# VectorE's order in a graph convolution, mixing weights without their zero columns

## The chip, the cores and the metric

The kernel runs on one core of a Trainium2 chip. The metric is the device time of one execution in microseconds (us); three runs of the kernel before took 1550.62, 1556.21 and 1556.63, median 1556.21. A profile was taken of another execution.

## The reference, cut to what matters

The model has two layers. Each is a convolution on a graph of 512 nodes, with three low-rank attentions, followed by a feed-forward part (experts in layer 0, ternary weights in layer 1). For each of 16 batch items, with x of 512 nodes, 16 channels and 12 times:

```python
x_res = _conv2d(jnp.swapaxes(x, 1, 2), res_w, res_b, STRIDE, 0)
xc = ...
xt = ...
s = _attention(xt, W1_s, W2_s, False)
h = jnp.einsum('bnm,bmct->bnct', s * A[None], xt)
g = jnp.einsum('bnct,cf->bnft', h, W_gcn)
y = _conv2d(jnp.swapaxes(g, 1, 2), tcn_w, tcn_b, STRIDE, 1) + x_res
y = jax.nn.relu(y)
z = jnp.transpose(y, (0, 3, 2, 1))
mu = z.mean(-1, keepdims=True)
var = ((z - mu) ** 2).mean(-1, keepdims=True)
z = (z - mu) / jnp.sqrt(var + 1e-05) * ln_g + ln_b
```

`xc` and `xt` are attentions over channels and over times. `s` is a softmax over 512 scores per node. The convolution `tcn_w` has three taps in time, so an output time depends on its own input time and on the one before and after it.

## The kernel before, in words

A layer's stage for all this is `graph_conv` (line 796). It is called once per layer and handles the 16 batch items in turns; `item_turns` (line 858) lists them from -1 to 17, with a hardware loop for the middle ones. Each engine has its own `turn` (TensorE line 940, VectorE line 1054, ScalarE line 1163), which is the hand-written order of its queue. An engine executes its queue in order, and semaphores alone tie the engines together. In turn b three items are in work at once: the softmax and the spreading of item b, the projections and first scores of item b+1, and the layer norm of item b-1. The residual of item b-2 is added on the way.

One item passes through these steps:

- VectorE builds a Kronecker matrix of the two small attentions (`kron_matrix`). TensorE multiplies it by `s.wm` (`kron_weights`, L882). `s.wm` has 96 partitions, two halves h of the 192 rows (time, channel), and 254 columns: 62 projection columns, then 192 mixing columns (12 output times of 16 channels). The rows of half 0 are times 0 to 5, those of half 1 times 6 to 11. Since a tap reaches one time to either side, half 0 has mixing columns other than zero for the output times 0 to 6 only, half 1 for 5 to 11 only. ScalarE copies the product to `kw` (`copy_kw`, L1125).
- TensorE projects the item (`projections`, L892); ScalarE and VectorE split the result in a high and a low part (`high_uv`, L1132; `split_uv`, L1014). TensorE convolves the item in four slabs of 128 nodes (`conv_slab`, L903); ScalarE copies them out (`copy_z`, L1137). The last two slabs wait for `split_uv`, because they share its PSUM bank.
- For each of four blocks k of 128 nodes: TensorE forms 128x512 scores (L912), VectorE takes the row maximum (`row_max`, L983), ScalarE the exponential and its sum (`row_exp`, L1143), VectorE the reciprocal and the product with the adjacency (`row_probs`, L990 and L992), TensorE transposes the result (`turn_probs`, L920), ScalarE copies it (`copy_turned`, L1151), and TensorE spreads the item over the nodes (`spread`, L931 and L935). Scores 0 and 1 of item b+1 are formed in turn b already.
- Layer norm: ScalarE applies the relu (L1156). VectorE takes the means and centres (`centre`, L1024 to L1027), ScalarE squares (L1161), and VectorE sums the squares and makes a first guess at the reciprocal root (`variance`, L1033 to L1039). GpSimd improves the guess in three steps of four instructions (L1104 to L1107), each waiting for the one before. VectorE multiplies by the root (`divide`, L1045), GpSimd by the gain (L1114), and VectorE adds the residual (L1051), to which GpSimd had added the bias (L1097).

Every VectorE and GpSimd step in such a chain waits for its predecessor by a semaphore (`Chain`). `divide` waits for GpSimd's root and is the last of VectorE's turn. The weights `s.wm` are loaded (`conv_loads`, line 165), scaled (`prepare`, line 213) and filled (`mix`, line 248) in the stage before, where they are spread over its batch items.

Of the kernel before, what the change touches and what calls it, by code (L numbers as in the profile page):

```python
# [28 lines left out]
O = 16  # L29
# [9 lines left out]
HALF = CT // 2  # L39
TH = T // 2  # L40
# [124 lines left out]
def conv_loads(eng, s, d, L, loaded):  # L165
# [6 lines left out]
        (s.wm[:, :, 0:NPROJ], p("ws").rearrange("(h p) r -> p h r", p=HALF)),  # L172
# [26 lines left out]
class ConvWeights:  # L199
# [13 lines left out]
    def prepare(self, dve):  # L213
# [4 lines left out]
        nc.vector.tensor_scalar(s.wm[:, :, 0:KR], s.wm[:, :, 0:KR], 1.0 / float(np.sqrt(np.float32(CT))), None, ALU.mult)  # L218
# [29 lines left out]
    def mix(self, h, dt):  # L248
        nc, s, step = self.nc, self.s, self.step
        rows = lambda x, n: x.unsqueeze(1).to_broadcast([HALF, n, O])  # L250
        mask = s.tmask[:, h, dt, :].unsqueeze(2).to_broadcast([HALF, T, O])
        tap = rows(self.mixed[:, h, O * dt:O * dt + O], T)
        mix = s.wm[:, h, NPROJ:NPROJ + CT].rearrange("p (t o) -> p t o", t=T)
        tm = self.small[0:HALF, 480:480 + CT].rearrange("p (t o) -> p t o", t=T)
# [541 lines left out]
def graph_conv(nc, s, tag, xn_rows, x_in, prefetch=None):  # L796
# [5 lines left out]
    with ExitStack() as ctx:  # L802
# [21 lines left out]
        with nc.Block() as block:  # L824
# [46 lines left out]
            def _(pe):  # L871
# [4 lines left out]
                def kron_weights(b, q):  # L876

                    pe.wait_ge(kron_done, ready(b))
                    pe.wait_ge(z_sb, ready(b - 1))
                    for ho in range(2):  # L880
                        for h in range(2):
                            last = nc.tensor.matmul(psz[0:HALF, 0, (NPROJ + CT) * ho:(NPROJ + CT) * (ho + 1)],  # L882
                                                    kron[q][0:HALF, h, HALF * ho:HALF * ho + HALF], s.wm[:, h, :],
                                                    start=(h == 0), stop=(h == 1))
                    last.then_inc(kw_done, 1)

                def projections(b, q, i):
                    pe.wait_ge(kw_sb, ready(b))
                    pe.wait_ge(xn_in[q], dma_ready(i))
                    for h in range(2):  # L890
                        for j in range(2):
                            last = nc.tensor.matmul(psz[UV * j:UV * j + UV, 1, 0:NODES], kw[q][0:HALF, h, 0:UV],  # L892
                                                    xnT[q][0:HALF, h, NODES * j:NODES * j + NODES],
                                                    start=(h == 0), stop=(h == 1))
                    last.then_inc(uv_done, 1)

                def conv_slab(b, q):
                    pe.wait_ge(kw_sb, ready(b))
                    for k in range(NK):
                        if k == 2:  # L900
                            pe.wait_ge(uv_sb, ready(b))
                        for h in range(2):
                            last = nc.tensor.matmul(psz[:, k // 2, CT * (k % 2):CT * (k % 2) + CT],  # L903
                                                    xnT[q][0:HALF, h, P * k:P * k + P], kw[q][0:HALF, h, NPROJ:],
# [69 lines left out]
            def _(dve):  # L974
# [45 lines left out]
                def centre(b, q):  # L1020
# [4 lines left out]
                    step(nc.vector.tensor_scalar(s.mu[:, :, :], s.mu[:, :, :], 1.0 / O, None, ALU.mult))  # L1025
                    dve.wait_ge(gained, free(b, 2))
# [27 lines left out]
                def turn(b, q, i, softmax=True, project=True, norm=True, kron=True, total=True):  # L1054
# [3 lines left out]
                    if norm:  # L1058
                        centre(b - 1, r)
                    if softmax:  # L1060
                        row_probs(b, 2)
                        row_max(b, 3)
                    if project:
# [3 lines left out]
                    if total:  # L1067
                        residual(b - 2, q)
                    if norm:
                        variance(b - 1, r)  # L1070
                    if project:
                        row_max(b + 1, 0)
# [1515 lines left out]
```

## Time and profile before

| | us |
|---|---|
| three runs, median | 1556.21 |
| three runs, lowest and highest | 1550.62 and 1556.63 |
| profiled execution, its own time | 1545.26 |
| profiled execution, span from first to last instruction | 1543.4 |
| TensorE busy, share of the span | 1320.0, 86% |
| VectorE busy | 968.8, 63% |
| ScalarE busy | 685.1, 44% |
| GpSimd busy | 592.6, 38% |

The two graph convolutions take a good part of the span, roughly from 134 to 425 us (layer 0) and from 1095 us to 1385 us (layer 1). The trace calls the engines PE (TensorE; PEld is its weight load), DVE (VectorE), ACT (ScalarE), POOL (GpSimd) and SP (the queue of DMAs). Buffers are named without their numbers: `L_rstd` is the layer's `rstd`, `g_s` the stage's PSUM tile for scores. A TensorE matmul of float32 appears as two records, a transposition as one. Matmuls are pipelined: the distance from one group's start to the next says what the group costs, and the duration of the last record runs on beyond that. The mean granted clock of TensorE over the span was 0.918.

### The profile page before, as it was taken

How to read it: one execution, taken by the hardware profiler on the slowest of the kernel's cores; microseconds unless marked ns; L12 is line 12 of the kernel's file. 1: busy time of each engine (PE TensorE's matmuls, PEld its weight loads, DVE VectorE, ACT ScalarE, POOL GpSimd, SP SyncE). 2: the span in 40 equal slices, each digit the busy share in tenths (PEclk: the TensorE clock that was granted, in tenths of full speed). 3: DMA queues.
4: the chain of work that ended last, by engine and by line, in shares of the span. 5: the costliest groups of instructions: out<-in, count | busy, mean ns of one | idle time of the engine just before them, and what ended most of it. 6: DMA issues, size and time to landing. Idle time of an engine off the chain costs nothing. (4 is left out here: it accounts for less than half of the span.)

```text
span 1543.4 us, 25763 instructions
## 1 busy us (share of the span) xinstructions
PE 1320.0 (86%) x8314; PEld 1113.2 (72%) x8330; DVE 968.8 (63%) x2091; ACT 685.1 (44%) x1195; POOL 592.6 (38%) x904
## 2 busy tenths in 40 slices
PE   6787999999494899999999994677899999937997
PEld 5686888888493788888888883657698888834554
DVE  4412788888667646444644432647378888857895
ACT  5422555555274333233323322523255554426996
POOL 1100266566620464664466432100036566560000
PEclk9788999999886799999999996578899999977999
DMA  7471011111075354655465616975111111100111
GB/s 239 124 212 47 22 52 51 43 53 46 21 227 167 92 127 110 150 85 132 110 148 87 121 20 168 303 239 163 42 32 52 42 52 49 51 11 11 46 48 62
DMA packets 86321, 148.81 MB, mean 96 GB/s; under 512 B 13907, under 2 KB 31971, under 8 KB 86247
## 3 DMA queue, kind: packets, MB, share of 16 engines
q1 hardware_dynamic: 63975, 103.78, 21.9%
q0 software_dynamic: 16384, 31.51, 11.9%
q10 hardware_dynamic: 5888, 12.59, 2.4%
q8 instruction: 41, 0.67, 0.2%
q14 instruction: 33, 0.27, 0.1%
HBM read 94.32 MB, written 53.51 MB: 96 GB/s over the span
## 5 line engine op out<-in xcount | busy, mean ns | idle before, releaser
L935 PE MATMUL g_y<-L_z,L_pt 128*128 128x192 f32 x1024 | 193.8, 332 | 26.6 <-ACT L_pt L1151 26.5
L935 PEld LDWEIGHTS g_y<-L_z,L_pt 128*128 128x128 f32 x1024 | 163.4, 190 | 32.5 <-ACT L_pt L1151 32.5
L1097 POOL TENSOR_TENSOR L_xr<-L_xr,L_lnb 128x192 f32<-128x192 f32 x128 | 105.7, 853 | 169.3 <-DMA L_xr<-x 88.9
L1143 ACT ACTIVATE L_e<-g_s,L_nm 128x512 f32<-128x512 f32 x128 | 87.9, 687 | 161.7 <-DVE L_nm L983 160.7
L1492 POOL DMA_INDIRECT sums<-x_yo,x_places x64 | 102.9, 1608 | 135.4 <-ACT x_yo L1731 125.3
L1621 DVE TENSOR_TENSOR x_mid<-ex_g,x_sig 128x480 f32<-128x480 f32 (+1 forms) x48 | 31.4, 654 | 119.4 <-ACT x_sig L1722 119.4
L1104 POOL TENSOR_TENSOR L_t<-L_rstd 128x48 f32<-128x48 f32 x96 | 29.1, 303 | 196.4 <-DVE L_rstd L1039 191.4
L992 DVE SCALAR_TENSOR_TENSOR L_p<-L_e,L_rl,L_adj 128x512 f32<-128x512 f32 x128 | 99.2, 775 | 4.5
L983 DVE TENSOR_REDUCE L_nm<-g_s 128x1 f32<-128x512 f32 x128 | 87.5, 683 | 15.7 <-PE g_s L912 14.9
L1477 POOL DMA_INDIRECT x_xin<-xn_rows,x_index x64 | 64.5, 1007 | 72.6 <-DVE x_index L1591 39.1
L903 PE MATMUL g_z<-L_kw,L_xnT 96*128 96x192 f32 x512 | 88.5, 325 | 0.0
L931 PEld LDWEIGHTS g_y<-L_res,L_xnT 97*128 97x128 f32 x512 | 74.4, 191 | 17.9 <-issue 11.5
L1114 POOL TENSOR_TENSOR L_d<-L_d,L_lng 128x192 f32<-128x192 f32 x128 | 73.1, 602 | 34.3 <-DVE L_d L1045 34.3
L1151 ACT ACTIVATE L_pt<-g_t 128x512 f32<-128x512 f32 x128 | 75.7, 592 | 22.6 <-PE g_t L920 19.3
L920 PE MATMUL g_t<-s_ident,L_p 128*128 128x128 f32 x512 | 77.4, 274 | 6.0 <-DVE L_p L992 6.0
L903 PEld LDWEIGHTS g_z<-L_kw,L_xnT 96*128 96x128 f32 x512 | 82.0, 189 | 0.5
L931 PE MATMUL g_y<-L_res,L_xnT 97*128 97x96 f32 x512 | 77.7, 274 | 0.7 <-ACT L_y L1156 0.7
L1700 ACT ACTIVATE x_xh<-ex_t 128x480 fp32r<-128x480 f32 x64 | 35.9, 569 | 94.7 <-PE ex_t L1520 94.7
L1548 PE MATMUL ex_d<-x_wdh,x_hh 128*120 128x512 f32 (+1 forms) x192 | 77.6, 404 | 0.0
L1722 ACT ACTIVATE x_sig<-ex_g 128x480 f32<-128x480 f32 (+1 forms) x48 | 27.4, 570 | 111.6 <-PE ex_g L1534 111.6
L1731 ACT ACTIVATE x_yo<-ex_d,x_gate 120x512 f32<-120x512 f32 x64 | 44.0, 688 | 73.6 <-PE ex_d L1548 73.6
L1534 PE MATMUL ex_g<-x_xh,x_guh 128*128 128x480 f32 (+1 forms) x192 | 75.7, 394 | 0.9 <-DVE x_xl L1600 0.9
(351 smaller groups left out, 3474.1 us busy)
## 6 DMA issues: line engine op xcount, KB each, us to landing
L_xnT<-xn_rows SPq DMA_DIRECT2D x48, 384.0 KB, 3.4
xn_rows<-L_xnT SPq DMA_DIRECT2D x54, 192.0 KB, 3.3
L_xr<-in_x SPq DMA_DIRECT2D x24, 384.0 KB, 3.1
L_raw<-xn_rows SPq DMA_DIRECT2D x16, 384.0 KB, 5.3
L_xr<-x SPq DMA_DIRECT2D x16, 384.0 KB, 3.1
out_x<-ff_yo SPq DMA_DIRECT2D x16, 384.0 KB, 2.6
s_gu<-in_Wg SPq DMA_DIRECT2D x8, 704.0 KB
s_gu<-in_Wu SPq DMA_DIRECT2D x8, 704.0 KB
```

Source lines behind the costliest of these rows:

```text
L903: last = nc.tensor.matmul(psz[:, k // 2, CT * (k % 2):CT * (k % 2) + CT], xnT[q][0:HALF, h, P * k:P * k + P], kw[q][0:HALF, h, NPROJ:], st ...
L920: last = nc.tensor.transpose(pst[k % 2][:, P * c:P * c + P], pr[k % 2][:, P * c:P * c + P], s.ident[:, :])
L931: nc.tensor.matmul(out[:, HALF * h:HALF * h + HALF], xnT[q][0:HALF + 1, h, P * k:P * k + P], s.res[0:HALF + 1, h, :], start=(h == 0), stop ...
L935: last = nc.tensor.matmul(out, pt[k % 2][:, P * c:P * c + P], z[q][:, c, :], start=False, stop=(c == NK - 1))
L983: nc.vector.tensor_reduce(s.nm2[:, k % 2:k % 2 + 1], pss[k % 2][:, :], AX, ALU.max, negate=True).then_inc(nmax_done, 1)
L992: nc.vector.scalar_tensor_tensor(out=pr[k % 2][:, :], in0=e[k % 2][:, :], scalar=s.rl[:, k % 2:k % 2 + 1], in1=s.adj[:, k, :], op0=ALU.mul ...
L1097: last = nc.gpsimd.tensor_tensor(v_, v_, gain(s.lnb), ALU.add)
L1143: nc.scalar.activation(e[k % 2][:, :], pss[k % 2][:, :], ACT.Exp, bias=s.nm2[:, k % 2:k % 2 + 1], accum_out=s.l[:, k % 2:k % 2 + 1]).then_ ...
L1151: nc.scalar.activation(pt[k % 2][:, :], pst[k % 2][:, :], ACT.Copy).then_inc(probs_turned_sb, 1)
L1492: nc.gpsimd.indirect_dma_start(sums, row(places[e % 2][:, 1, t:t + 1]), yo[t % 4][:, :], None, compute_op=ALU.add).then_inc(sent[t % 4], 16)
L1534: last = nc.tensor.matmul(ps_[z][0:size, 0:SN], w[:, k, off + at:off + at + size], x[q][:, k, SN * c:SN * c + SN], start=(k == 0 and x is ...
L1548: last = nc.tensor.matmul(psd[t % 2][0:ST, :], h[0:size, j, ST * t:ST * t + ST], w[0:size, j, :], start=(j == 0 and h is hh and w is wdh), ...
```

## The change

The diff does three things.

On VectorE, `centre` is parted in `means` (the sum and its scaling) and `centre` (the subtraction), and the latter is moved behind the third `row_probs` and the fourth `row_max`. The first `row_max` of the next item is moved from behind `variance` to ahead of it, directly behind `residual`.

The columns of `s.wm` and `kw` change places: 96 mixing columns (times 0 to 5), 62 projection columns, 96 mixing columns (times 6 to 11). So the columns that half 0 reaches are the first 174, and those that half 1 reaches are the last 174, with 94 in common. `kron_weights` issues three matmuls for each half of the output in place of two, 174, 94 and 80 columns wide. `projections` and `conv_slab` read their columns from the new places, the latter as two runs of 96. Both buffers get 316 columns for each half in place of 254, so that the two runs lie a fixed step apart. `mix` writes them so, with one dimension more in its patterns.

On TensorE, the order of the calls in `turn` is as before.

```diff
+NKW = CT + NPROJ
+SPAN = HALF + NPROJ
+REACH = SPAN + O
...
-        (s.wm[:, :, 0:NPROJ], p("ws").rearrange("(h p) r -> p h r", p=HALF)),
+        (s.wm[:, :, HALF:SPAN], p("ws").rearrange("(h p) r -> p h r", p=HALF)),
...
-        mask = s.tmask[:, h, dt, :].unsqueeze(2).to_broadcast([HALF, T, O])
-        tap = rows(self.mixed[:, h, O * dt:O * dt + O], T)
-        mix = s.wm[:, h, NPROJ:NPROJ + CT].rearrange("p (t o) -> p t o", t=T)
-        tm = self.small[0:HALF, 480:480 + CT].rearrange("p (t o) -> p t o", t=T)
+        halves = lambda x: x.rearrange("p (a t) -> p a t", a=2)
+        mask = halves(s.tmask[:, h, dt, :]).unsqueeze(3).to_broadcast([HALF, 2, TH, O])
+        tap = self.mixed[:, h, O * dt:O * dt + O].unsqueeze(1).unsqueeze(1).to_broadcast([HALF, 2, TH, O])
+        mix = halves(s.wm[:, h, :])[:, :, 0:HALF].rearrange("p a (t o) -> p a t o", t=TH)
+        tm = self.small[0:HALF, 480:480 + CT].rearrange("p (a t o) -> p a t o", a=2, t=TH)
...
-                        for h in range(2):
-                            last = nc.tensor.matmul(psz[0:HALF, 0, (NPROJ + CT) * ho:(NPROJ + CT) * (ho + 1)],
-                                                    kron[q][0:HALF, h, HALF * ho:HALF * ho + HALF], s.wm[:, h, :],
-                                                    start=(h == 0), stop=(h == 1))
+                        for h, lo, hi, start, stop in ((0, 0, REACH, True, False), (1, HALF - O, REACH, False, True),
+                                                       (1, REACH, NKW, True, True)):
+                            last = nc.tensor.matmul(psz[0:HALF, 0, NKW * ho + lo:NKW * ho + hi],
+                                                    kron[q][0:HALF, h, HALF * ho:HALF * ho + HALF], s.wm[:, h, lo:hi],
+                                                    start=start, stop=stop)
...
-                                                    xnT[q][0:HALF, h, P * k:P * k + P], kw[q][0:HALF, h, NPROJ:],
+                                                    xnT[q][0:HALF, h, P * k:P * k + P], taps(kw[q], h),
...
-                def centre(b, q):
+                def means(b, q):
 
                     step.begin(b * NORM_STEPS)
                     dve.wait_ge(relu_done, ready(b))
                     step(nc.vector.tensor_reduce(flat(s.mu), oct_(y[q]), AX, ALU.add))
                     step(nc.vector.tensor_scalar(s.mu[:, :, :], s.mu[:, :, :], 1.0 / O, None, ALU.mult))
+
+                def centre(b, q):
+
                     dve.wait_ge(gained, free(b, 2))
                     step(nc.vector.tensor_tensor(oct_(dv[q]), oct_(y[q]), lanes(s.mu), ALU.subtract))
...
                     if norm:
-                        centre(b - 1, r)
+                        means(b - 1, r)
                     if softmax:
                         row_probs(b, 2)
                         row_max(b, 3)
+                    if norm:
+                        centre(b - 1, r)
                     if project:
                         split_uv(b + 1, r)
                     if softmax:
                         row_probs(b, 3)
                     if total:
                         residual(b - 2, q)
+                    if project:
+                        row_max(b + 1, 0)
                     if norm:
                         variance(b - 1, r)
                     if project:
-                        row_max(b + 1, 0)
                         row_probs(b + 1, 0)
                         row_max(b + 1, 1)
```

## Rows read from the trace of the kernel before

**Rows 1.** Windows: us busy (x instructions) per engine, then TensorE's granted clock, DMA

```profile
320.00:350.00 30.00, 28.15 (x184) 25.51 (x184) 26.24 (x53) 15.57 (x33) 17.21 (x38) 1.00 0.17 52
1520.00:1540.00 20.00, 13.71 (x92) 7.70 (x92) 8.96 (x18) 11.47 (x12) 0.00 (x0) 1.00 0.16 56
```

**Rows 2.** Who waited for whom, 183-392 us: total us, times, longest

```profile
PE g_y L935 <- ACT L_pt L1151: 10.3, 12, 0.9
...
DVE L_d L1045 <- POOL L_rstd L1107: 2.3, 13, 0.2
```

**Rows 3.** VectorE's timeline, one turn: start, us, line, operation [idle before, releaser]

```profile
199.49 0.96 DVE L1045 TENSOR_TENSOR L_d<-L_d,L_rstd 128x768 f32<-128x768 f32 x1 [0.18 <-POOL L_rstd L1107]
200.37 0.68 DVE L983 TENSOR_REDUCE L_nm<-g_s 128x1 f32<-128x512 f32 x1
200.97 0.94 DVE L1024 TENSOR_REDUCE L_mu<-L_y 128x48 f32<-128x768 f32 x1
...
202.30 1.29 DVE L1027 TENSOR_TENSOR L_d<-L_y,L_mu 128x768 f32<-128x768 f32 x1
...
207.94 0.95 DVE L1051 TENSOR_TENSOR s_shared<-L_d,L_xr 128x768 f32 x1
208.81 0.94 DVE L1033 TENSOR_REDUCE L_var<-L_sqr 128x48 f32<-128x768 f32 x1
...
210.32 0.19 DVE L1039 TENSOR_SCALAR L_rstd<-L_guess 128x48 int32<-128x48 int32 x1
...
212.16 0.17 DVE L990 RECIPROCAL L_rl<-L_l 128x1 f32<-128x1 f32 x1 [0.92 <-ACT L_e L1143]
212.36 0.85 DVE L992 SCALAR_TENSOR_TENSOR L_p<-L_e,L_rl,L_adj 128x512 f32<-128x512 f32 x1
...
214.93 0.75 DVE L992 SCALAR_TENSOR_TENSOR L_p<-L_e,L_rl,L_adj 128x512 f32<-128x512 f32 x1
215.86 0.96 DVE L1045 TENSOR_TENSOR L_d<-L_d,L_rstd 128x768 f32<-128x768 f32 x1 [0.18 <-POOL L_rstd L1107]
```

**Rows 4.** GpSimd's timeline, same turn

```profile
210.59 0.27 POOL L1104 TENSOR_TENSOR L_t<-L_rstd 128x48 f32<-128x48 f32 x1 [4.46 <-DVE L_rstd L1039]
...
212.74 0.61 POOL L1106 TENSOR_TENSOR L_t<-s_c,L_t 128x48 f32<-128x48 f32 x1
...
215.01 0.82 POOL L1107 TENSOR_TENSOR L_rstd<-L_rstd,L_t 128x48 f32<-128x48 f32 x1
```

**Rows 5.** TensorE's timeline, same turn and the start of the next

```profile
208.38 0.53 PE L912 MATMUL g_s<-L_v,L_u 128*128 128x512 f32 x1
...
211.17 0.58 PE L931 MATMUL g_y<-L_res,L_xnT 97*128 97x96 f32 x4
212.67 1.57 PE L935 MATMUL g_y<-L_z,L_pt 128*128 128x192 f32 x8 [0.92 <-ACT L_pt L1151]
...
214.74 1.88 PE L882 MATMUL g_z<-L_wm,L_k 96*96 96x254 f32 x8
216.46 0.58 PE L931 MATMUL g_y<-L_res,L_xnT 97*128 97x96 f32 x4
216.88 1.49 PE L935 MATMUL g_y<-L_z,L_pt 128*128 128x192 f32 x8
```

**Rows 6.** VectorE's timeline in turn 1

```profile
175.92 0.95 DVE L1033 TENSOR_REDUCE L_var<-L_sqr 128x48 f32<-128x768 f32 x1
...
177.87 0.69 DVE L983 TENSOR_REDUCE L_nm<-g_s 128x1 f32<-128x512 f32 x1 [0.24 <-PE g_s L912]
```

**Rows 7.** TensorE's timeline, start of the stage and turn 1

```profile
135.79 3.59 PE L882 MATMUL g_z<-L_wm,L_k 96*96 96x254 f32 x8
...
177.30 0.53 PE L912 MATMUL g_s<-L_v,L_u 128*128 128x512 f32 x1
```

**Rows 8.** VectorE's timeline at the stage's end, itself idle beside the iteration

```profile
410.06 0.96 DVE L1045 TENSOR_TENSOR L_d<-L_d,L_rstd 128x768 f32<-128x768 f32 x1 [4.33 <-POOL L_rstd L1107]
```

**Rows 9.** Line L259: duration ns min/median/max, first and last start, forms

```profile
L259 DVE TENSOR_TENSOR L_wm<-L_wm,L_y x8: 353/354/357, 52.9 to 1016.4; 96x192 f32<-96x192 f32 x8
```

More of the change, by code:

```diff
@@ L217, in prepare @@
         dve.wait_ge(self.loaded, 16 * CONV_LOADS)
-        nc.vector.tensor_scalar(s.wm[:, :, 0:KR], s.wm[:, :, 0:KR], 1.0 / float(np.sqrt(np.float32(CT))), None, ALU.mult)
+        nc.vector.tensor_scalar(s.wm[:, :, HALF:HALF + KR], s.wm[:, :, HALF:HALF + KR], 1.0 / float(np.sqrt(np.float32(CT))), None, ALU.mult)
         nc.vector.tensor_copy(self.lhs_g.rearrange("p (t c) -> p t c", t=T),
@@ L891, in projections @@
                         for j in range(2):
-                            last = nc.tensor.matmul(psz[UV * j:UV * j + UV, 1, 0:NODES], kw[q][0:HALF, h, 0:UV],
+                            last = nc.tensor.matmul(psz[UV * j:UV * j + UV, 1, 0:NODES], kw[q][0:HALF, h, HALF:HALF + UV],
                                                     xnT[q][0:HALF, h, NODES * j:NODES * j + NODES],
@@ L895, in projections, with taps @@
                     last.then_inc(uv_done, 1)
+                def taps(w, h):
+                    return w[0:HALF, h, :].rearrange("p (a x) -> p a x", a=2)[:, :, 0:HALF]
                 def conv_slab(b, q):
@@ L1124, in copy_kw @@
                     act.wait_ge(z_done, free(b, 2))
-                    nc.scalar.activation(kw[q][0:HALF, :, :],
-                                         psz[0:HALF, 0, 0:2 * (NPROJ + CT)].rearrange("p (h x) -> p h x", h=2),
+                    nc.scalar.activation(kw[q][0:HALF, :, 0:NKW],
+                                         psz[0:HALF, 0, 0:2 * NKW].rearrange("p (h x) -> p h x", h=2),
                                          ACT.Copy).then_inc(kw_sb, 1)
@@ L2327, in conv_buffers @@
     s.wt = sb("wt", [P, NK, C, PROJ])
-    s.wm = sb("wm", [HALF, 2, NPROJ + CT])
+    s.wm = sb("wm", [HALF, 2, 2 * SPAN])
     s.res = sb("res", [P, 2, HALF])
@@ L2359, in conv_buffers @@
     s.k1 = sb("k1", [P, 2, CT])
-    s.kw0 = sb("kw0", [P, 2, NPROJ + CT])
-    s.kw1 = sb("kw1", [P, 2, NPROJ + CT])
+    s.kw0 = sb("kw0", [P, 2, 2 * SPAN])
+    s.kw1 = sb("kw1", [P, 2, 2 * SPAN])
     s.u0 = sb("u0", [P, N], F32R)
```

## The prediction

> **What bounds the kernel now.** I read the windows first, because the change touches one stage only, the graph convolution, which runs once in each of the two layers. In a steady stretch TensorE is busy for 28.15 of 30 us and VectorE for 26.24 [rows 1], so by busy time TensorE looks like the limit, with VectorE close behind. The reader should not stop there: two engines this close to full mean that a loop through both, or through VectorE and a third engine, may set the period. The waits tell which. Over the steady part of layer 0, TensorE waited 12 times for the turned probabilities, 0.9 us each, and VectorE waited 13 times out of 13 for GpSimd's `L_rstd` ahead of the division on L1045, 0.2 us each [rows 2]. The long wait draws the eye. The short one decides, as VectorE's timeline shows.
>
> One turn handles one batch item. It goes from a division at 199.49 to the next at 215.86: a period of 16.37 us [rows 3]. Take VectorE from the division on: row maximum, means, centring, probabilities, maximum, splitting, probabilities, residual, variance, and the seed of the root, which ends at 210.32 + 0.19 = 210.51. In these 11.02 us VectorE waits for nobody. GpSimd waits 4.46 us for that seed, starts its three-step root iteration at 210.59 and ends it at 215.01 + 0.82 = 215.83 [rows 4]. The division starts 0.03 us later. So 11.02 us of VectorE and 5.35 us of GpSimd (and two hand-overs) close a ring, and 11.02 + 5.35 is the whole period. Everything else has slack: under the iteration VectorE idles 0.92 us [rows 3], and TensorE idles 0.92 us before the fourth spread at 212.67 [rows 5]. The latter waits for a copy that stands on ScalarE behind the exponential of the next item's scores, which waits for that item's row maximum behind the variance. That is the wait which the change goes for. It is not in the ring.
>
> **The change, part by part.** *The next row maximum ahead of the variance.* Before, this maximum ran after the seed, beside the iteration, and cost the ring nothing. Now it stands inside the 11.02 us. VectorE's maxima follow one another at 0.60 us start to start (200.37 to 200.97) [rows 3]. It also has to wait for its score. TensorE starts that score at 208.38 [rows 5]; in turn 1, where VectorE visibly waits for such a score, the maximum starts 0.57 us after it (177.87 against 177.30) [rows 6, 7]. 208.38 + 0.57 = 208.95 against 208.81, when the variance starts now [rows 3]: 0.14 us of waiting. I keep that value: the slabs ahead of the score wait for VectorE's splitting, which is in the ring too, so the score moves with it. Together 0.60 + 0.14 = 0.74 us per turn. Queued behind the waiting maximum are the variance, GpSimd's iteration and the division.
>
> *The iteration itself.* With the maximum gone from its start, the first probability instruction begins right after the seed. Which instructions slow GpSimd is seen in the rows: most of its 128x48 steps take 0.27 to 0.29 us, but the one at 215.01 takes 0.82 while VectorE's 128x512 product of 214.93 runs, and the one at 212.74 takes 0.61 beside that of 212.36 [rows 3, 4]. At the stage's end, with VectorE idle, seed to division is 4.33 us of waiting [rows 8], against 5.35 here. So about 1.0 us of the iteration is such blocking. After the change the same two products and the two small ones of the Kronecker matrix still fall into it, so I keep 5.35 and add 0.06 for a worse alignment of the first; the bounds are one product more or less in the way, about 0.35 us either way.
>
> The Trainium skill's page "SBUF — State Buffer", section "Who interferes with whom", says the same of the pair: a VectorE instruction with two SBUF inputs and a GpSimd instruction that reads SBUF block each other entirely, in order of issue, and a VectorE reduction does not contend. It speaks against this change, since moving a reduction out of the iteration frees GpSimd of nothing; by it the sum stays as it is here, and the trace's 0.82 beside 0.28 agrees.
>
> *Centring parted from the means.* The subtraction goes behind the third probabilities and the fourth maximum, but stays within the same 11.02 us, so its place costs nothing. Its duration is 1.29 us against 0.96 for the division of the same size [rows 3], because GpSimd works beside it. In the new place GpSimd still does; if it did not, 0.3 us would go, and if the product now in front is slowed too, 0.3 come. I take 0. Its square on ScalarE needs to be done only by the variance, with the splitting, a pair of probabilities and the residual in between.
>
> *Fewer columns in the mixing weights.* Per turn, 4 matmuls of 254 columns become 2 each of 174, 94 and 80: 1016 columns to 696. The four now take 216.46 - 214.74 = 1.72 us, 0.43 each. By columns the six would take 1.18 us, a saving of 0.54. But two matmuls of 96 columns take 216.88 - 216.46 = 0.42, 0.21 each, which is more than their columns' share, so at that width something else than the columns sets the pace [rows 5]. With that floor the six take 2 x (0.295 + 0.21 + 0.21) = 1.43, a saving of 0.29. I take 0.3, the nearer row. In the steady turns it is off the ring and worth nothing: TensorE only waits longer. The copies of these weights and the slabs read and write the same number of elements in two runs; the slabs' matmuls are off the ring too, with some 2 us of TensorE's slack as cover.
>
> *Turn 1 and the start.* Before turn 1 nothing of the ring runs, and TensorE is the limit. There the smaller matmuls do help: the first set takes 3.59 us [rows 7]; 17% (0.29 of 1.72) of that and of its successors is about 1.4 us by turn 1. Against this, the variance of turn 1 started at 175.92, while the next maximum had to wait for TensorE until 177.87 [rows 6]. Now it must wait for it: 177.87 - 1.4 + 0.60 = 177.07, 1.15 us later. Bounds: none (saving by columns) to 2 us (no saving).
>
> *The rest.* The instructions that build the weights get one more dimension in their pattern: 20 of some 0.35 us, such as the eight at 0.354 [rows 9]; were they a quarter slower or faster, 1.8 us in all. The weight load has the same bytes. Both 0.
>
> **Sum.** The ring closes with a moved maximum in turns 2 to 14: 13 per layer. 0.74 + 0.06 = 0.80 us, times 13 is 10.4, plus 1.15 is 11.55 per layer, 23.1 for two. The profiled execution took 1545.3 us (span 1543.4) and would take 1568. It lies 10.9 us below the median of the runs, 1556.2; against that median I forecast **1579 us**, 1.5% slower.
>
> **Rivals.** *Faster: TensorE is the bound.* If the ring were not closed, TensorE's wait of 0.92 us goes and 0.3 us of matmuls with it: 1.2 x 26 = 32 us, 1524. For it: 28.15 of 30 us busy [rows 1], and the wait does end as the change intends. It decides if GpSimd's root is there before VectorE asks for it. Against it: VectorE waited for it in every turn [rows 2]. Chance 0.09. The Trainium skill's page "Perfetto Trace Analysis", section "Identifying the Most-Contended Engine", would have one optimise the engine of highest occupancy first, which is this rival, though it warns that matmul busy time is no good measure.
>
> *No change: the iteration gets shorter.* With VectorE done early and idle before the division, GpSimd's blocking of about 1.0 us might vanish: 0.74 - 1.02 = -0.28 per turn, -7 us, with turn 1 about -5: 1551; with half of it gone, 0.23 x 26 + 2 = 8: 1564. Against it: the products still lie inside. Chance 0.12.
>
> *Slower still: the score is late.* The maximum is issued as soon as TensorE has the score, and if TensorE, which now waits longer before the projections, is 0.5 us later with it, each turn loses 1.3 us: 34 + 2 = 36, 1592. TensorE's order after the projections has no more waits in view, so 0.10.
>
> *That the change is not what it says.* The words name an exchanged order on TensorE; in the diff TensorE's turn is unchanged, and only columns change places. No time hangs on it. Also a slower clock is no case for me: the granted clock was 1.00 with TensorE busy only 13.71 of 20 us [rows 1].
>
> **Chances and range.** The forecast has 0.69. With the late score, slower is 0.79; no change 0.12; faster 0.09, the line being 0.5% (7.8 us), about what a measurement of this kernel can tell from no change. Its own range: 0.80 less 0.35 in the iteration and nothing at turn 1 gives 12 us, 1568; 1.15 and 2 us give 34, 1590. To hold 8 in 10 it reaches down into the no-change case: 1554 to 1592.
>
> **What would show it.** Right: the period from division to division goes to about 17.2 us; VectorE's wait for `L_rstd` grows from 0.18 to about 1.8 us (5.4 less some 3.6 of work and waiting in between), and its 0.92 us wait for the exponential is gone; GpSimd's wait for the seed grows from 4.46 to about 5.2; TensorE no longer waits before the fourth spread but some 2 us before the projections, for ScalarE's copy of the weights, which stands behind the maximum after the division; the mixing matmuls need about 1.43 us for six. Wrong: a period at or below 16.4 us, or a division that finds its root waiting. The size is wrong if the maximum's wait for its score differs from 0.14 us or seed to division from 5.4.

## The result: slower, by more than forecast

| | median us (range, executions) | before, on the same chip | ratio, 95% interval |
|---|---|---|---|
| changed kernel | 1593.68 (1590.33 to 1596.77, 4) | 1553.41 | 1.0263, 1.0222 to 1.0303 |
| forecast | 1579 (1554 to 1592) | 1556.21 | 1.015 |

The kernel became slower, as forecast, but by 40 us in place of 23, and its time lies 1.7 us above the range. The profiled execution took 1594.34 us with a span of 1592.5, so 49.1 us more than the one before. (Of two kernels below, three executions above 1610 us, with mean granted clocks of 0.884 to 0.888, are left out of ratios, medians and ranges as slow runs; what made them slow is not known.)

The changed kernel's VectorE, one turn from division to division and the same maximum in a later turn: start, us, line, operation, and in brackets the idle time before it with its releaser.

```profile
216.38 0.96 DVE L1057 TENSOR_TENSOR L_d<-L_d,L_rstd 128x768 f32<-128x768 f32 x1 [1.98 <-POOL L_rstd L1122]
...
220.73 1.30 DVE L1039 TENSOR_TENSOR L_d<-L_y,L_mu 128x768 f32<-128x768 f32 x1
222.25 0.47 DVE L1023 SCALAR_TENSOR_TENSOR L_u<-L_uvh,s_lowmask,g_z 30x256 fp32r<-30x256 f32 x1 [0.23 <-DVE L_d L1039]
...
225.09 0.95 DVE L1063 TENSOR_TENSOR s_shared<-L_d,L_xr 128x768 f32 x1
226.18 0.69 DVE L992 TENSOR_REDUCE L_nm<-g_s 128x1 f32<-128x512 f32 x1
226.78 0.94 DVE L1045 TENSOR_REDUCE L_var<-L_sqr 128x48 f32<-128x768 f32 x1
...
228.30 0.19 DVE L1051 TENSOR_SCALAR L_rstd<-L_guess 128x48 int32<-128x48 int32 x1
...
233.84 0.96 DVE L1057 TENSOR_TENSOR L_d<-L_d,L_rstd 128x768 f32<-128x768 f32 x1 [1.99 <-POOL L_rstd L1122]
...
300.19 0.69 DVE L992 TENSOR_REDUCE L_nm<-g_s 128x1 f32<-128x512 f32 x1 [3.06 <-PE g_s L921]
```

This answers to [rows 3]. The period is 233.84 - 216.38 = 17.46 us, 1.09 more. VectorE's part of the ring, division to seed, is 228.49 - 216.38 = 12.11 us against 11.02. The 1.09 are 0.60 for the maximum (226.18 to 226.78), 0.22 because it starts 1.09 us after the residual where the variance used to start 0.87 after it, 0.26 because the residual itself starts 8.71 us after the division in place of 8.45, and 0.01 behind it. Of the 0.26, 0.19 are a gap: the splitting starts 0.22 us after the centring's end (222.03), where in the kernel before the probabilities followed it after 0.03 (202.30 + 1.29 = 203.59, then this line of its VectorE timeline, same turn as [rows 3]):

```profile
203.62 0.16 DVE L990 RECIPROCAL L_rl<-L_l 128x1 f32<-128x1 f32 x1
```

Seed to division is 233.84 - 228.49 = 5.35 us, the same as before (in five turns of layer 1 it is 5.15; the plain ones among them take 17.2 us). GpSimd's side answers to [rows 4]:

```profile
228.57 0.27 POOL L1119 TENSOR_TENSOR L_t<-L_rstd 128x48 f32<-128x48 f32 x1 [5.54 <-DVE L_rstd L1051]
```

It now waits 5.54 us for the seed, where it waited 4.46.

TensorE's timeline, the same plain turn and then a slow one, against [rows 5]:

```profile
219.36 1.08 PE L897 MATMUL g_z<-L_xnT,L_kw 96*64 96x256 f32 x8 [1.94 <-ACT L_kw L1140]
...
225.52 0.53 PE L921 MATMUL g_s<-L_v,L_u 128*128 128x512 f32 x1
...
228.92 1.57 PE L944 MATMUL g_y<-L_z,L_pt 128*128 128x192 f32 x8
...
231.00 1.42 PE L887 MATMUL g_z<-L_wm,L_k 96*96 96x174 f32 x12
232.26 0.62 PE L940 MATMUL g_y<-L_res,L_xnT 97*128 97x96 f32 x4
...
290.46 1.88 PE L897 MATMUL g_z<-L_xnT,L_kw 96*64 96x256 f32 x8 [1.95 <-ACT L_kw L1140]
...
293.24 2.82 PE L944 MATMUL g_y<-L_z,L_pt 128*128 128x192 f32 x8
...
299.53 0.53 PE L921 MATMUL g_s<-L_v,L_u 128*128 128x512 f32 x1
...
300.32 1.49 PE L944 MATMUL g_y<-L_z,L_pt 128*128 128x192 f32 x8
```

The wait ahead of the fourth spread (228.92) is gone, and one of 1.94 us stands ahead of the projections. The mixing matmuls take 232.26 - 231.00 = 1.26 us against 1.72. The lower half shows what the forecast had ruled out: behind the same wait, eight spread records take 2.82 us in place of 1.49, and from the start of the projections to that of the score it is 9.07 us in place of 6.16. The windows of four whole turns show why (length, then us busy and instructions of TensorE, its weight load, VectorE, ScalarE and GpSimd, then granted clock, DMA share, GB/s):

```profile
233.84:251.27 17.43, 15.37 (x106) 13.84 (x105) 14.43 (x28) 8.43 (x17) 9.99 (x20) 1.00 0.14 45
268.73:287.48 18.75, 16.77 (x106) 15.48 (x105) 14.41 (x28) 8.46 (x17) 9.98 (x20) 0.91 0.14 42
287.48:307.86 20.38, 18.39 (x106) 16.51 (x105) 14.42 (x29) 8.28 (x17) 9.97 (x20) 0.83 0.14 39
387.68:405.11 17.43, 15.37 (x106) 13.85 (x105) 14.43 (x29) 8.44 (x17) 9.98 (x20) 1.00 0.15 45
```

All four do the same work. In a plain turn the granted clock is 1.00 throughout; in the longer turns a part runs at the lower of TensorE's two levels (1.2 and 2.4 GHz). The clock is back at the higher level by the end of the turn (300.32: 1.49 us again), but the moved maximum has waited 3.06 us for its score by then, with the seed and the division behind it. The whole excess of such a turn stands there: the maximum starts up to 4.05 us after the residual in place of 1.09, and seed to division stays at 5.35 to 5.39 us in layer 0. The waits of the whole stretch (us in total, times, longest), against [rows 2]:

```profile
PE g_z L897 <- ACT L_kw L1140: 23.2, 12, 2.0
DVE L_d L1057 <- POOL L_rstd L1122: 21.8, 11, 2.0
...
DVE L_nm L992 <- PE g_s L921: 16.6, 7, 3.1
```

**Where the 49.1 us went.** I part each stage at its first mixing matmul and at the 16 divisions:

| us | before | changed | difference |
|---|---|---|---|
| ahead of the first mixing matmul | 135.79 | 129.73 | -6.06 |
| layer 0: first mixing matmul to first division | 47.22 | 50.44 | +3.22 |
| layer 0: first to last division | 238.63 | 267.40 | +28.77 |
| between the layers | 675.57 | 678.34 | +2.77 |
| layer 1: first mixing matmul to first division | 44.89 | 50.91 | +6.02 |
| layer 1: first to last division | 238.71 | 253.13 | +14.42 |

Most of it, 43.2 us, lies between first and last division. The two layers do the same work there and differ by 14 us, mainly because layer 0 has seven turns of 18.7 to 20.4 us, layer 1 only two above 18.

### The profile page after: what moved, and what is told of

The parts are those of the page before. It is cut to its first block and busy times, and to the rows that moved or that the text cites. A ratio compares the mean times of both kernels' runs of the same rounds, so it can differ in the third digit from the quotient of the medians.

```text
span 1592.5 us, 26003 instructions
## 1 busy us (share of the span) xinstructions
PE 1336.7 (84%) x8442; PEld 1131.3 (71%) x8458; DVE 968.8 (61%) x2091; ACT 687.8 (43%) x1195; POOL 592.3 (37%) x904
## 5 line engine op out<-in xcount | busy, mean ns | idle before, releaser
L944 PE MATMUL g_y<-L_z,L_pt 128*128 128x192 f32 x1024 | 207.3, 349 | 8.5 <-ACT L_pt L1166 7.4
L944 PEld LDWEIGHTS g_y<-L_z,L_pt 128*128 128x128 f32 x1024 | 175.2, 201 | 14.4 <-ACT L_pt L1166 14.4
L1119 POOL TENSOR_TENSOR L_t<-L_rstd 128x48 f32<-128x48 f32 x96 | 25.7, 268 | 249.6 <-DVE L_rstd L1051 244.6
L912 PE MATMUL g_z<-L_kw,L_xnT 96*128 96x192 f32 x512 | 95.7, 335 | 1.4
L912 PEld LDWEIGHTS g_z<-L_kw,L_xnT 96*128 96x128 f32 x512 | 85.4, 196 | 6.4 <-DVE L_v L1023 6.4
L940 PEld LDWEIGHTS g_y<-L_res,L_xnT 97*128 97x128 f32 x512 | 75.1, 199 | 17.2 <-issue 13.4
L929 PE MATMUL g_t<-s_ident,L_p 128*128 128x128 f32 x512 | 81.2, 284 | 4.7 <-DVE L_p L1001 4.7
L940 PE MATMUL g_y<-L_res,L_xnT 97*128 97x96 f32 x512 | 82.4, 285 | 0.6 <-ACT L_y L1171 0.6
L897 PE MATMUL g_z<-L_xnT,L_kw 96*64 96x256 f32 x256 | 37.9, 420 | 49.2 <-ACT L_kw L1140 49.2
```

Source lines behind the costliest of these rows:

```text
L929: last = nc.tensor.transpose(pst[k % 2][:, P * c:P * c + P], pr[k % 2][:, P * c:P * c + P], s.ident[:, :])
L940: nc.tensor.matmul(out[:, HALF * h:HALF * h + HALF], xnT[q][0:HALF + 1, h, P * k:P * k + P], s.res[0:HALF + 1, h, :], start=(h == 0), stop ...
L944: last = nc.tensor.matmul(out, pt[k % 2][:, P * c:P * c + P], z[q][:, c, :], start=False, stop=(c == NK - 1))
```

## The experiments

Theory: the ring of VectorE's 11 us and GpSimd's 5.35 sets the period; whatever is added between division and seed costs its duration. Rivals: TensorE's new wait and clock are the whole loss, or the centring or the weights cost something by themselves.

**Each part alone.** `max_only` is the kernel before with the maximum moved:

```diff
+                    if project:
+                        row_max(b + 1, 0)
                     if norm:
                         variance(b - 1, r)
                     if project:
-                        row_max(b + 1, 0)
                         row_probs(b + 1, 0)
```

> The kernel before with one edit: the next item's first row maximum ahead of the variance. Ring theory (VectorE from division to seed, then GpSimd's iteration, sets the turn): the steady turn goes from 16.37 to about 17.2 us (0.60 for the maximum, about 0.2 for its wait for the score), VectorE waits about 1.8 us for the root, TensorE waits about 1.5 us ahead of the projections: 21 us by the ring, about 1575; if that idle time also lets TensorE's clock fall in some turns, as it did in 13 to 14% of the changed kernel's stage, up to 18 us more. Rival, the loss comes from the narrower matmuls or the parted centring: no loss here, 1545 to 1555.

`centre_only` is the kernel before with `means` and `centre` parted and placed as in the change:

```diff
                     if norm:
-                        centre(b - 1, r)
+                        means(b - 1, r)
                     if softmax:
                         row_probs(b, 2)
                         row_max(b, 3)
+                    if norm:
+                        centre(b - 1, r)
```

> The kernel before with the centring parted from the means and moved behind the fourth maximum. Ring theory: the splitting now stands right behind the centring, and in the changed kernel it starts 0.2 us late there in the turns of the hardware loop: period 16.57, 12 turns a layer, 5 us: about 1558. Rival, the place of the centring is free: 1553, period 16.37.

`weights_only` is the changed kernel with VectorE's turn of before, so its diff to the kernel before is the columns' part of the change alone:

```diff
+                        for h, lo, hi, start, stop in ((0, 0, REACH, True, False), (1, HALF - O, REACH, False, True),
+                                                       (1, REACH, NKW, True, True)):
...
```

> The kernel before with the narrower mixing weights alone, VectorE's order as before. Ring theory: the matmuls are off the ring; the period stays 16.37 and TensorE waits 0.46 us longer in a turn; only the start of a stage gains, about 1 us each: 1551. Rival A (TensorE bounds the turn): 26 turns by 0.46, 12 us faster: 1541. Rival B (six small matmuls, or the reads in two runs, cost more than they save): slower than 1560.

| | median us (range, n) | ratio to before, 95% | plain turn in layer 0, us |
|---|---|---|---|
| before | 1547.99 (1542.04 to 1555.63, 19) | | 16.37 |
| max_only | 1577.55 (1573.63 to 1582.56, 4) | 1.0208, 1.0179 to 1.0238 | 17.18 |
| centre_only | 1551.27 (1545.25 to 1556.95, 10) | 1.0018, 0.9996 to 1.0040 | 16.62 |
| weights_only | 1551.28 (1549.43 to 1557.32, 10) | 1.0029, 1.0016 to 1.0042 | 16.38 |

The three parts add up: 16.37 + 0.81 + 0.25 + 0.01 = 17.44 us, against 17.43 measured. The maximum alone makes the root late (VectorE's two divisions, then TensorE's projections in the `max_only` timeline):

```profile
218.65 0.96 DVE L1045 TENSOR_TENSOR L_d<-L_d,L_rstd 128x768 f32<-128x768 f32 x1 [1.98 <-POOL L_rstd L1108]
...
235.83 0.96 DVE L1045 TENSOR_TENSOR L_d<-L_d,L_rstd 128x768 f32<-128x768 f32 x1 [1.98 <-POOL L_rstd L1108]
...
221.63 1.08 PE L892 MATMUL g_z<-L_xnT,L_kw 96*64 96x256 f32 x8 [1.52 <-ACT L_kw L1126]
```

In `centre_only` the division's wait stays at 0.18 us, the period is 228.12 - 211.47 = 16.65 in this turn, and VectorE stands still for 0.23 us between the centring and the splitting (VectorE's timeline):

```profile
211.47 0.96 DVE L1048 TENSOR_TENSOR L_d<-L_d,L_rstd 128x768 f32<-128x768 f32 x1 [0.18 <-POOL L_rstd L1112]
...
215.83 1.29 DVE L1030 TENSOR_TENSOR L_d<-L_y,L_mu 128x768 f32<-128x768 f32 x1
217.35 0.47 DVE L1014 SCALAR_TENSOR_TENSOR L_u<-L_uvh,s_lowmask,g_z 30x256 fp32r<-30x256 f32 x1 [0.23 <-DVE L_d L1030]
...
228.12 0.96 DVE L1048 TENSOR_TENSOR L_d<-L_d,L_rstd 128x768 f32<-128x768 f32 x1 [0.18 <-POOL L_rstd L1112]
```

In `weights_only` TensorE saves its 0.46 us of mixing matmuls and waits as before ahead of the fourth spread, here 0.93 us, and 0.22 us ahead of the projections:

```profile
229.46 1.57 PE L944 MATMUL g_y<-L_z,L_pt 128*128 128x192 f32 x8 [0.93 <-ACT L_pt L1160]
```

Still it is 0.3% slower than the kernel before, and the interval is clear of no change. Its turns do not show this; outside them, the stretch between the layers is 681.66 us in its trace against 675.57. Over all traces that stretch is 675.6 to 678.0 us in the three kernels with the old columns and 678.3 to 681.7 in the ten traces with the new ones. So the columns may cost a little outside the ring; which instruction pays it was not found (the weight-building instructions of [rows 9] are not it: 0.355 us each in the changed kernel, 0.354 before).

**The splitting's hold.** In `after_no_hold` the centring stays in its place and still raises its semaphore, for ScalarE's square, but VectorE's queue no longer waits for its end:

```diff
-                    step(nc.vector.tensor_tensor(oct_(dv[q]), oct_(y[q]), lanes(s.mu), ALU.subtract))
+                    nc.vector.tensor_tensor(oct_(dv[q]), oct_(y[q]), lanes(s.mu), ALU.subtract).then_inc(stats_done, 1)
```

> The changed kernel, where VectorE does not wait for its own centring before the splitting (the semaphore is still raised, and later waits of the same chain cover it). In the hardware loop the splitting starts 0.2 us after the centring, in the turns outside the loop 0.04. Theory: the splitting's waits take register values in the loop, which are worked out only after the centring's own wait is over; without that wait the 0.2 us go: turns of 17.2 us in place of 17.43, 24 turns, 5 us. Rival (GpSimd's work or the centring's late end holds the splitting): turns stay 17.43.

```profile
224.58 1.29 DVE L1039 TENSOR_TENSOR L_d<-L_y,L_mu 128x768 f32<-128x768 f32 x1
225.79 0.46 DVE L1023 SCALAR_TENSOR_TENSOR L_u<-L_uvh,s_lowmask,g_z 30x256 fp32r<-30x256 f32 x1
...
237.36 0.96 DVE L1057 TENSOR_TENSOR L_d<-L_d,L_rstd 128x768 f32<-128x768 f32 x1 [1.97 <-POOL L_rstd L1122]
```

The splitting now starts 0.08 us before the centring's end, and the turn is 17.12 us, 0.31 less: the hold was the centring's price. The total missed: 1592.56 us median (1574.62 to 1595.12, 3), ratio 1.0352 (1.0301 to 1.0404), no better than the changed kernel, which had 1.0354 beside the same runs of the kernel before (`after_again` below). The profiled execution was the shortest, with one turn of 18.93 and one of 18.67; the two others had mean granted clocks of 0.902 and 0.900 against its 0.913. So a shorter turn did not help, and the clock is the likely reason. It is not shown, since the two others have no trace, and the mean clock is a weak sign: one execution of the changed kernel had 0.865 and took 1596.77 us, another 0.906 and 1594.34.

**The clock.** `after_filled` puts seven matmuls whose product nobody reads into TensorE's wait ahead of the projections; nothing else changes:

```diff
                         scores(b, q, 3)
+                    if softmax and project and norm:
+                        keep_awake(nc, s, psy[:, 0, 384:512], 7)
                     if project:
                         projections(b + 1, r, i + 1)
```

> The changed kernel with seven idle 128x128 matmuls (into unused PSUM columns) ahead of the projections, where TensorE waits 1.94 us per turn. Clock theory (that wait lets TensorE's clock fall to its lower level, and turns with it take up to 20.4 us in place of 17.4): the granted clock is 1.00 in all steady turns, all take 17.4 us, about 18 us go: about 1576. Rival (the clock falls for reasons that the idle time does not set): as the changed kernel, about 1594, turns of 18.7 to 20.4 us remain.

It took 1583.84 us (1580.03 to 1586.62, 4), ratio 1.0236 (1.0205 to 1.0267), 8 us above the expectation. The wait shrank to 0.36 us (TensorE's timeline):

```profile
223.22 1.08 PE L897 MATMUL g_z<-L_xnT,L_kw 96*64 96x256 f32 x8 [0.36 <-ACT L_kw L1142]
```

All middle turns then took 17.40 to 17.51 us in layer 0 and 17.20 to 17.46 in layer 1; none was slow. First to last division are 251.54 and 250.30 us in place of 267.40 and 253.13, which is 18.7 less for the two layers. In the ratios less of it is seen (1.0236 against 1.0263, timed at different times), and the two spans differ by 10.5 us only (1582.0 against 1592.5): 7.2 us went back in the stretches ahead of the first mixing matmul and between the layers, which vary from trace to trace. So both ran once more, each beside the kernel before (`after_again` is the changed kernel itself, `filled_again` is `after_filled`):

> The changed kernel once more, unchanged, for its turns and its clock in a second trace. Clock theory: the plain turn is 17.43 us again; some turns, not necessarily the same ones, take 18.5 to 20.4 us at a granted clock of 0.83 to 0.91; 1590 to 1597. Rival (the slow turns were a peculiarity of that one execution): all turns 17.4 us, about 1576 to 1580.

> The changed kernel with the seven idle matmuls once more. Clock theory: all its runs lie close together, none with slow turns, 1580 to 1587, ratio 1.022 to 1.026, where the changed kernel by itself ran from 1590 to 1624. Rival (the runs of the changed kernel spread for another reason): the filled kernel spreads as far.

`after_again`: 1601.87 us (1593.79 to 1605.47, 4), ratio 1.0354 (1.0323 to 1.0386), above what was expected. Its slow turns are others than in the first trace: of layer 0's fifteen the fourth to eighth and tenth to thirteenth, where it had been the first and the sixth to eleventh. `filled_again`: 1583.07 (1577.71 to 1583.91, 6), ratio 1.0222 (1.0196 to 1.0249). The steady stretch of layer 0 in windows, first of `after_again`:

```profile
180.00:420.00 240.00, 214.21 (x1311) 193.85 (x1309) 182.30 (x352) 104.87 (x214) 126.24 (x252) 0.90 0.14 41
```

and of `filled_again`:

```profile
180.00:420.00 240.00, 230.03 (x1601) 210.29 (x1600) 198.21 (x386) 115.39 (x235) 139.01 (x280) 1.00 0.14 43
```

More matmuls on TensorE made the kernel faster: in the same 240 us VectorE got 386 instructions done in place of 352. The filled kernel's ratio repeats (1.0236, 1.0222); the changed kernel's does not (1.0263, 1.0354, intervals apart). What the clock takes is thus not one number: by the ratios 0.3% to 1.3% of the time, by the two profiled executions 18.7 and 22.6 us (both against `after_filled`). These runs were on several chips (`after_filled` on one, `after_again` on another, `filled_again` on a third), so how much of that spread is the chip's was not told apart.

**The other side of the ring.** If GpSimd's iteration is half of it, shortening it must pay one to one. `after_two_steps` is the changed kernel with two refinements of the root in place of three; it leaves out the third:

```diff
-                        chain.begin(b * 11)
+                        chain.begin(b * 7)
...
-                        for n in range(3):
+                        for n in range(2):
...
-                            if n < 2:
+                            if n < 1:
```

> The changed kernel with two of the three steps of GpSimd's root iteration (leaves out the third refinement). Ring theory: the iteration is in the ring, 4 instructions at 0.36 us start to start go, 1.45 us of VectorE's 1.98 us wait for the root: turns of 17.43 - 1.45 = 16.0 us, TensorE's wait ahead of the projections falls by as much, to 0.5 us, and its clock stays up: 26 turns by 1.45 is 38 us plus up to 18 of the clock, 1540 to 1556. Rival (VectorE and TensorE alone set the turn): as the changed kernel, 1594.

```profile
216.36 0.96 DVE L1057 TENSOR_TENSOR L_d<-L_d,L_rstd 128x768 f32<-128x768 f32 x1 [0.54 <-POOL L_rstd L1122]
...
232.37 0.96 DVE L1057 TENSOR_TENSOR L_d<-L_d,L_rstd 128x768 f32<-128x768 f32 x1 [0.54 <-POOL L_rstd L1122]
...
219.34 1.08 PE L897 MATMUL g_z<-L_xnT,L_kw 96*64 96x256 f32 x8 [0.49 <-ACT L_kw L1140]
```

The turn is 232.37 - 216.36 = 16.01 us, 1.42 less, and the wait for the root 0.54, 1.45 less. TensorE's wait is 0.49 us and the granted clock 1.00. The time is 1534.16 us (1531.61 to 1535.24, 4), ratio 0.9918 (0.9898 to 0.9938): the only edit is on GpSimd, and it takes back the whole loss.

**Taking VectorE's work out of the ring.** `early_variance` has the weights of the change and, in VectorE's order of before, the variance and the maximum ahead of the residual, which takes 0.87 us out of the ring:

```diff
-                    if total:
-                        residual(b - 2, q)
                     if norm:
                         variance(b - 1, r)
                     if project:
                         row_max(b + 1, 0)
+                    if total:
+                        residual(b - 2, q)
+                    if project:
                         row_probs(b + 1, 0)
```

> The kernel before with the narrower mixing weights and another order on VectorE: variance first, then the next row maximum, then the residual (before: residual, variance, maximum). Ring theory: the residual's 0.87 us leave the part between division and seed, nothing enters it: 11.02 - 0.87 = 10.15, plus 5.35 for the iteration, plus up to 0.4 if the residual, now beside the iteration, blocks GpSimd: turns of 15.5 to 15.9 us, 13 to 23 us faster than the kernel before (ratio 0.985 to 0.992). The maximum comes 0.9 us earlier, so TensorE's wait ahead of the fourth spread goes too. Rival (TensorE or VectorE as a whole bounds the turn): 16.37 us stay, ratio 1.00.

1543.24 us (1540.43 to 1545.70, 11), ratio 0.9978 (0.9961 to 0.9995): the turn went to 16.18 us, by 0.2 only, where 15.5 to 15.9 was expected. VectorE's seed, its residual and the division, then one of GpSimd's steps:

```profile
236.53 0.19 DVE L1048 TENSOR_SCALAR L_rstd<-L_guess 128x48 int32<-128x48 int32 x1
...
237.36 0.95 DVE L1060 TENSOR_TENSOR s_shared<-L_d,L_xr 128x768 f32 x1
...
242.74 0.96 DVE L1054 TENSOR_TENSOR L_d<-L_d,L_rstd 128x768 f32<-128x768 f32 x1 [0.91 <-POOL L_rstd L1117]
...
237.50 0.94 POOL L1116 TENSOR_TENSOR L_t<-s_c,L_t 128x48 f32<-128x48 f32 x1
```

Seed to division is now 242.74 - 236.72 = 6.02 us, 0.67 longer. Beside the residual a step of GpSimd takes 0.94 in place of some 0.28. The Trainium skill's page "SBUF — State Buffer", section "Who interferes with whom", says that a VectorE instruction with two SBUF inputs contends with a GpSimd instruction that reads SBUF; these rows agree. So what leaves the ring on VectorE's side can come back on GpSimd's: of the residual's 0.87 us, 0.67 did. The maximum, a reduction, left the iteration in `max_only` without shortening it: seed to division stayed at 5.35 us.

**Opening the ring.** The division need not be the last of its turn. In `defer_after` (on `after_no_hold`) it moves to the next turn, behind the third probabilities; `defer_before` does the same on `weights_only`, with VectorE's old order:

```diff
                         row_probs(b, 2)
+                    if total:
+                        divide(b - 2, q)
+                    if softmax:
                         row_max(b, 3)
...
-                    if norm:
-                        divide(b - 1, r)
```

> The changed kernel, without the wait behind the centring, and with the division by the root put off to the next turn, behind its third probabilities: the iteration then has VectorE's maximum, means and probabilities of the next turn beside it as well, 6.3 us against the 5.35 it takes. Ring theory: the ring is open, VectorE never waits for the root, and a turn is what VectorE needs by itself: 17.12 (the changed kernel without that wait) less 1.98 of waiting = 15.1, or what TensorE needs, 15.0; with waits between the two 15.2 to 15.6 us, 26 turns by 0.8 to 1.2, 20 to 30 us below the kernel before: ratio 0.981 to 0.987. Rival (another wait of the same size stands behind the root): 16 us or more, ratio 0.99 to 1.0.

> The narrower mixing weights with VectorE's order of the kernel before, and the division put off to the next turn in the same way. Ring theory: VectorE's wait of 0.18 us for the root goes, but its 0.92 us wait for the exponential (maximum behind the variance) stays in its own sequence: 16.37 - 0.18 = 16.2 us, 5 us faster, ratio 0.997. So the moved maximum is worth something once the ring is open: this kernel stays 0.6 us a turn or more behind the other one. Rival (the maximum's place never matters): both kernels alike.

`defer_after`: **1521.98 us** (1519.59 to 1525.47, 6), ratio **0.9831** (0.9807 to 0.9855), faster than both kernels. `defer_before`: 1544.59 (1539.06 to 1546.86, 12), ratio 0.9974 (0.9953 to 0.9995). In `defer_after`'s timeline the root is ready 0.63 us ahead of the division, and VectorE waits for neither root nor score:

```profile
218.10 0.95 DVE L1057 TENSOR_TENSOR L_d<-L_d,L_rstd 128x768 f32<-128x768 f32 x1
...
233.29 0.95 DVE L1057 TENSOR_TENSOR L_d<-L_d,L_rstd 128x768 f32<-128x768 f32 x1
...
232.37 0.29 POOL L1123 TENSOR_TENSOR L_rstd<-L_rstd,L_t 128x48 f32<-128x48 f32 x1
...
218.26 1.08 PE L897 MATMUL g_z<-L_xnT,L_kw 96*64 96x256 f32 x8
...
227.44 1.57 PE L944 MATMUL g_y<-L_z,L_pt 128*128 128x192 f32 x8
```

The turn is 233.29 - 218.10 = 15.19 us, and TensorE waits neither ahead of the projections nor of the fourth spread. VectorE's queue now stands still only for one exponential per turn, 0.30 us; TensorE is as full (16.97 of 17.00 us from 217 to 234), so which of the two sets these turns is open. In `defer_before` the wait behind the late maximum is the limit, and its middle turns are 16.01 to 16.12 us: besides this wait, VectorE's queue has no gap. Waits in the steady stretch (190 to 380 us: us in total, times, longest), first VectorE for the exponentials in `defer_after`, then in `defer_before`, there with TensorE's for the turned probabilities:

```profile
DVE L_rl L999 <- ACT L_e L1159: 3.6, 12, 0.3
...
DVE L_rl L999 <- ACT L_e L1153: 14.9, 24, 0.9
PE g_y L944 <- ACT L_pt L1161: 11.9, 12, 1.1
```

VectorE's 14.9 - 3.6 = 11.3 us over 12 turns are 0.94 per turn, about what the two kernels' turns differ by. So the moved maximum does remove a real wait. With the division out of the ring, VectorE's new order (maximum moved, centring parted, no hold) is worth 16.05 - 15.19 = 0.86 us per turn; in the ring the same maximum costs 0.81.

## Why the prediction was right in direction and too small

**The ring.** Right. Seed to division stayed at 5.35 us (layer 0); the moved maximum cost 0.81 us per turn against 0.80 (0.22 of waiting for its score where 0.14 was forecast, and nothing in the iteration where 0.06 was); the division's wait became 1.99 against 1.8, GpSimd's 5.54 against 5.2, TensorE's ahead of the projections 1.94 against some 2. That VectorE and GpSimd close it is shown from both sides, by `max_only` and `after_two_steps`.

**"Centring parted from the means ... its place costs nothing ... I take 0."** Wrong, 0.25 us per turn. The durations were as assumed (1.30 and 1.29). What I had not looked at is who follows: in the old place the probabilities, in the new one the splitting, and that starts 0.22 us after the centring's end. `after_no_hold` shows that this gap is the price: without it the turn is 17.12 us, no more than with the moved maximum alone (17.18). With it the ring's term for the two layers, taken from the filled kernel, is (251.54 + 250.30) - (238.63 + 238.71) = 24.5 us, where the forecast had 2 x 10.4.

**"Also a slower clock is no case for me."** Wrong, and in the traces the largest miss: 18.7 us of the profiled execution. The step took [rows 1] (1.00 with TensorE busy 13.71 of 20 us) as proof that idle time does no harm. It shows one stretch of another stage. The same prediction named the new TensorE wait of 2 us per turn and costed it at nothing; with that wait filled the clock stays at 1.00 and no turn is lengthened. By the ratios the clock is worth 4 to 20 us, where the measured 40 us exceed the forecast 23 by 17. An estimate from the filled kernel's ratios (1.0222 and 1.0236 of 1553.41) is 1588 to 1590 us: without the loss the time would have lain just inside the range, and still well above 1579. The rival "the score is late" had the right victim, the maximum waiting for its score, with another cause: not TensorE's order but its clock, and in some turns only, by 1.3 to 3 us beyond the 0.22 of a plain turn.

**"Turn 1 and the start."** Too small: 1.15 us per layer forecast, 3.2 and 6.0 measured. The 1.4 us by which smaller matmuls should have helped did not show, since `weights_only` starts 0.6 and 1.4 us later than the kernel before (47.79 and 46.27). The starts of the other kernels lie between 47.2 and 52.1 us, whatever their order, so what part of the 9.2 is the change's is not settled. The clock differs here too: from the first mixing matmul to the first division it is 0.93 and 0.99 in the kernel before, 0.89 in both layers of the changed kernel and 0.89 and 0.91 in `weights_only`; but `centre_only`, with the old columns, has 0.92 and 0.89. Outside the steps that I costed, the stretch ahead of the first mixing matmul came out 6.06 us shorter and that between the layers 2.77 longer. The first lies anywhere between 129.7 and 136.2 us over the thirteen traces (129.73 and 132.73 for the changed kernel alone), so it varies by as much from execution to execution; the second may be the columns' (see `weights_only`), and no run here tells by what.

**Mixing weights.** 1.26 us for six matmuls, between the two bounds (1.18 by columns, 1.43 with a floor). Off the ring, as forecast: the turn stays at 16.38.

**The other rivals.** TensorE as the bound fell: it waited more, and less work for it brought nothing; the gain came from an order on VectorE. The Trainium skill's page "Perfetto Trace Analysis", section "Identifying the Most-Contended Engine", which the prediction named for this rival, would not have TensorE judged by its matmuls' busy time, but by its share of peak operations and by how busy its weight loads are. By the latter, 25.51 of 30 us against VectorE's 26.24 [rows 1], TensorE was not the fullest engine, so the page did not speak for the rival. The shorter iteration fell with seed to division at 5.35.

**What stays open.** Which turns lose the clock: each has the same 1.9 us wait, and some keep it; in the profiled execution of `after_no_hold`, with 1.8 to 2.1 us in every turn, only the first turn of each layer lost it. And why the splitting holds: inside the hardware loop the gap is 0.19 to 0.23 us, in turns 1 and 14, which are written out for themselves, 0.03 to 0.04 (in turn 14 the centring ends at 409.45 + 1.29 and the splitting starts at 410.78). In the loop the kernel has the waits that precede it compare with a register, outside with a constant. That this is the cause is only a guess: `after_no_hold` shows that the wait for the centring's end makes the gap, not why it does so in the loop alone.

## What to carry to other kernels

Follow the short wait that occurs in every turn before the long one: if it closes a loop over two engines, work moved into that loop costs its full duration (and any wait that it brings along), and what it was moved for is worth something only once the loop is open. Cost a new TensorE wait by what its clock may do, even on an engine with slack, and try filling it. When an instruction moves, look at its new successor as well as its own duration.

## What the hardware did that was not expected

- TensorE, busy 15.37 us of a plain turn's 17.43, lost its clock in some turns: after an idle 1.95 us, a mean of 0.83 over the turn and 2.95 us more time, with the higher level back before the turn's end. In `max_only`, where the wait is mostly 1.51 us, one turn of each layer was slow, 18.79 us behind a wait of 1.35 and 18.73 behind one of 1.51; with 0.89 (`early_variance`), 0.49 (`after_two_steps`) and 0.36 (`after_filled`) the clock of the steady stretch stayed at 1.00.
- The splitting, which needs nothing from the centring but waits for its end by a semaphore, started 0.19 to 0.23 us after that end in the loop and 0.03 to 0.04 outside. In the same loop of the kernel before, the probabilities behind the centring started after 0.03 (203.62).
- Twelve records of 174, 94 and 80 columns took 1.26 us where eight of 254 take 1.72: nearly their share by columns (1.18), and less than the pace of the 96-column records of [rows 5] had made me expect (1.43).
